# Attention: stacked queries and keys turned by transposing DMAs within SBUF, and a third PSUM bank for scores

## The chip, the cores and the metric

The kernel runs on one core of a Trainium2 chip. Its time is the device time of one execution in microseconds (us); the median of several runs is given. The engines are PE (TensorE, matrix products), DVE (VectorE), ACT (ScalarE), POOL (GpSimd) and SP (SyncE), which here only issues DMAs. SBUF and PSUM are the on-chip memories; PE writes its results to PSUM, which has banks of 2 KB for each of 128 partitions.

## What is computed

A model of four layers on x of shape (16, 256, 256): batch, position, channel. Each layer adds an attention and a feed-forward part. Three of the four attentions, and the self-attention inside the third feed-forward part, are computed by the same function of the kernel. Cut to what matters, each of them is

```
q = split_heads(query)                 # (16, heads, 256, D / heads)
k, v = split_heads(split(memory))
scores = einsum('bhqd,bhkd->bhqk', q, k) + mask or bias of the keys
weights = softmax(scores, axis=-1)
out = einsum('bhqk,bhkd->bhqd', weights, v)
```

with 16 heads of 16 channels or 8 heads of 32; the self-attention is causal.

## The kernel before

The program is a row of stages; each stage has its own buffers and a block in which every engine runs a program of its own, and engines wait for each other by counting semaphores. The change touches `attention_stage` alone, which runs four times: as stage l0a (16 heads, from ctx_2048; it also zeroes two arrays in memory, `clears`), l2a (8 heads), l2s (16 heads, causal) and l3a (8 heads). The calls are in `build`, `self_layer` and `projected_layer`.

The unit of work is a half batch h: 32 of them in each stage, with HALF = heads / 2 heads each (8 or 4). `slots()` is the clock by which all engines' programs are written: j counts half batches, i the head in it, and n = j * HALF + i the head overall. The order of work on an engine is fixed by it; the time at which something runs is set by the waits alone.

- **Stacking (POOL, `stack`).** Scores are to be exact to more than fp16, so each head's query is stacked as high part, high part again and low part, its key as high, low, high; after these 3 * dh rows stand two rows for the bias and one for the row's maximum. Together a head has 64 rows (16 heads) or 128 (8 heads). They lie in `qs` and `ks` (two buffers each), positions on the partitions.
- **Turning (PE, `turn`, L659 to 683).** The product needs these rows on the partitions. PE turns 128x128 blocks against an identity matrix into two PSUM banks, `MH_ps` (in the profile l0a_M and so on): 8 for the queries and 8 for the keys of each half batch, h = j + 2 (TURN_Q_AT and TURN_K_AT). DVE copies the queries (`copy_queries`, L768) into `qT`, ACT the keys (`copy_keys`, L723) into `kT`, at h = j + 1; both are rings of 6 buffers.
- **Scores (PE, `score`, L622)** go to one of two banks `S_ps`, 512 columns a head, and PE waits until the maxima of head n - 2 are done. DVE takes the maxima of the rows (`maxima`, L788; L784 where causal) into `mx`.
- **Maxima back.** Once h = j - 1 is complete, PE turns `mx` (L689), into the first of the two `MH_ps` banks, which it shares with the queries. DVE copies the result to `nmT` (L796), and SP moves it by one DMA (8 heads) or two (16 heads) into a row of `qT` (L513).
- **Scores again, transposed and less the maximum (PE, `scoreT`, L636)**, LAG = heads + 1 heads behind the first ones; ACT takes the exponential (L737), in the causal stage POOL cuts what lies above the diagonal (L581), PE weighs the values (L652) into `O_ps`, ACT copies the sums (L731), PE turns them back (L696), DVE divides (L805, L816).
- **SP's queue** is in the order of the program: the load of keys and values (`kv`, L499) of every second half batch, in l0a the two zeroing DMAs (L506), and the maxima's rows (L513), for which SP waits at each half batch.

## Time and profile before

| | us |
|---|---|
| median of 3 runs | 3162.87 |
| lowest and highest | 3162.02, 3163.29 |
| the profiled execution | 3166.49 |
| its span, first to last instruction | 3164.8 |

The profile is one execution. Its views: the page gives busy time of each engine over the whole span; the busy time by stretch gives the same for chosen intervals, with the clock granted to PE (1.00 is full speed) and the share of the 16 DMA engines' time; the groups of instructions give count, busy us in all and mean ns of one; the waits say which group stood idle until which other one was done. The stages lie at about 65 to 301 us (l0a), 1631 to 1812 (l2a), 1935 to 2156 (l2s) and 2836 to 3019 (l3a), first scores to last products. PEld is PE's weight load, SPq the issue of a DMA on SP. Matmuls overlap, so that the busy time of a group is less than its count times the mean.

### The profile page before, as it was taken

The numbers are of one execution on the slowest core, as the hardware profiler recorded it, in microseconds if no ns is written. First come the engines' busy times: TensorE is split into PE (matmuls) and PEld (weight loads), VectorE is DVE, ScalarE is ACT, GpSimd is POOL, SyncE is SP. The second block draws the span as 40 slices with busy tenths as digits, with TensorE's granted clock in tenths as the row PEclk, the third lists the DMA queues.
The fourth block names the chain that finished last, engine by engine and source line by source line (L and its number), as shares of the span: only waits on it lengthen the run. The fifth ranks groups of instructions, "written<-read, shape, count | busy, mean of one in ns | idle before, by whom it ended". The sixth has DMA issues, their size and how long they took to land. (4 is left out here: it accounts for less than half of the span.)

```text
span 3164.8 us, 57450 instructions
## 1 busy us (share of the span) xinstructions
PE 2533.4 (80%) x21340; PEld 1655.2 (52%) x21340; DVE 2163.2 (68%) x5536; ACT 1307.5 (41%) x2296; POOL 1030.3 (33%) x1446
## 2 busy tenths in 40 slices
PE   1998377999615358997989986897799999969982
PEld 1444264766514136996446553445466555656662
DVE  5997755666477435665578778997766545877767
ACT  1887343343112212332346664773222222356622
POOL 2452371100163520112656467872300000034330
PEclk9999698999857679999999987998799999989996
DMA  3331363233330324775631022100100000011001
GB/s 100 127 128 51 131 235 130 74 104 101 99 92 1 108 96 177 261 250 202 210 120 49 15 84 81 43 23 6 64 9 13 1 1 1 1 39 49 29 9 58
DMA packets 158280, 266.65 MB, mean 84 GB/s; under 512 B 23003, under 2 KB 106249, under 8 KB 151988
## 3 DMA queue, kind: packets, MB, share of 16 engines
q1 hardware_dynamic: 131316, 186.70, 17.8%
q0 software_dynamic: 17904, 76.23, 7.0%
q8 instruction: 172, 2.82, 0.4%
q10 hardware_dynamic: 8784, 0.04, 0.2%
q14 instruction: 104, 0.85, 0.1%
HBM read 174.99 MB, written 88.34 MB: 83 GB/s over the span
## 5 line engine op out<-in xcount | busy, mean ns | idle before, releaser
L1595 ACT ACTIVATE l2e_hf<-l2e_H 128x512 f32<-128x512 f32 x208 | 124.2, 597 | 381.9 <-PE l2e_H L1538 381.9
L1727 POOL TENSOR_TENSOR all_m_rstd<-all_m_sq,all_mhalf 128x8 f32<-128x8 f32 x24 | 39.6, 1650 | 558.7 <-DVE all_m_sq L1712 524.3
L1634 DVE CAST l2e_hh<-l2e_hf 128x512 f16<-128x512 f32 x208 | 92.7, 446 | 122.9 <-ACT l2e_hf L1595 108.7
L788 DVE TENSOR_REDUCE l0a_mx<-l0a_S 128x2 f16<-128x512 f32 x256 | 166.7, 684 | 12.3 <-PE l0a_S L622 10.0
L1538 PE MATMUL l0e_H<-l0e_xT,l0e_w 128*128 128x512 f16 x768 | 168.7, 382 | 0.0
L1538 PE MATMUL l2e_H<-l2o_hi,l2e_w 128*128 128x512 f16 x576 | 151.8, 382 | 15.8 <-DVE l2e_w L1610 15.8
L784 DVE CUSTOM_DVE_ANT_0 l2s_masked<-l2s_S,l2s_mq 128x128 f32<-128x128 f32 (+1 forms) x512 | 153.0, 349 | 16.3 <-PE l2s_S L622 12.1
L737 ACT ACTIVATE l0a_pf<-l0a_ST 128x512 f32<-128x512 f32 x256 | 146.2, 600 | 38.5 <-PE l0a_ST L636 37.4
L1538 PE MATMUL l1e_H<-l1e_xT,l1e_w 128*128 128x256 f16 (+1 forms) x1404 | 158.3, 274 | 3.0 <-DMA l1e_w<-packed,all_second_weight_row 3.0
L1538 PE MATMUL l2e_H<-l2e_hh,l2e_w 128*128 128x512 f16 x640 | 155.1, 379 | 0.0
L1636 DVE TENSOR_TENSOR l2e_hl<-l2e_hf,l2e_hh 128x512 f16<-128x512 f32 x208 | 147.3, 708 | 7.2
L1538 PEld LDWEIGHTS l1e_H<-l1e_xT,l1e_w 128*128 128x128 f16 (+1 forms) x1404 | 143.7, 107 | 15.1 <-DMA l1e_w<-packed,all_second_weight_row 3.3
L737 ACT ACTIVATE l2s_pf<-l2s_ST 128x384 f32<-128x384 f32 x256 | 118.6, 493 | 47.4 <-PE l2s_ST L636 42.9
L1595 ACT ACTIVATE l0e_hf<-l0e_H 128x512 f32<-128x512 f32 x128 | 76.4, 597 | 141.7 <-PE l0e_H L1538 141.7
L2698 POOL DMA_INDIRECT l1n_yb<-results,all_first_read x64 | 63.0, 985 | 203.9 <-POOLq L57 176.8
L1553 PE MATMUL l0e_Y<-l0e_w,l0e_hh 128*128 128x256 f16 x1024 | 124.7, 273 | 0.0
L1538 PEld LDWEIGHTS l0e_H<-l0e_xT,l0e_w 128*128 128x128 f16 x768 | 75.6, 98 | 90.1 <-issue 2.1
L788 DVE TENSOR_REDUCE l3a_mx<-l3a_S 128x2 f16<-128x512 f32 x128 | 88.1, 693 | 40.9 <-PE l3a_S L622 39.8
L581 POOL TENSOR_SCALAR_AFFINE_SELECT l2s_pf<-l2s_pf 128x256 f32<-128x256 f32 x256 | 101.1, 407 | 42.2 <-ACT l2s_pf L737 42.0
L1553 PE MATMUL l2e_Y<-l2e_w,l2e_hh 128*128 128x192 f16 x1024 | 109.4, 248 | 3.5 <-DVE all_x L1650 3.5
L622 PE MATMUL l0a_S<-l0a_kT,l0a_qT 64*128 64x256 f16 x512 | 97.6, 285 | 15.8 <-DVE l0a_mx L788 15.8
L788 DVE TENSOR_REDUCE l2a_mx<-l2a_S 128x2 f16<-128x512 f32 x128 | 87.4, 690 | 29.9 <-PE l2a_S L622 29.1
(706 smaller groups left out, 7262.0 us busy)
## 6 DMA issues: line engine op xcount, KB each, us to landing
l0e_wf<-in_L_ffn_w SPq DMA_DIRECT2D x16, 1024.0 KB, 8.7
rows<-l0a_zeros SPq DMA_DIRECT2D x16, 640.0 KB
l1e_rb<-rows SPq DMA_DIRECT2D x39, 256.0 KB, 8.8
results<-l1e_y SPq DMA_DIRECT2D x39, 256.0 KB, 2.2
l0a_kv<-in_ctx SPq DMA_DIRECT2D x16, 512.0 KB, 4.1
rows<-l0a_zeros SPq DMA_DIRECT2D x16, 512.0 KB
l0d_p_cx<-in_ctx SPq DMA_DIRECT2D x16, 512.0 KB, 7.5
l0e_rb<-rows SPq DMA_DIRECT2D x16, 512.0 KB, 9.7
```

The lines of the kernel that those rows point to most:

```text
L581: nc.gpsimd.affine_select(out=t, in_=t, compare_op=ALU.is_ge, fill=0.0, base=0, pattern=[[0, TB], [1, P]], channel_multiplier=-1).then_inc ...
L622: m = pe.matmul(S_ps[n % 2][:, s_at[u]:s_at[u] + key_to[u]], qT[h % RING][r0:r0 + rows, j, u * P:u * P + P], kT[h % RING][r0:r0 + rows, j, ...
L737: nc.scalar.activation(pf[n % NPF][:, 0:used], ST_ps[n % 2][:, 0:used], ACT.Exp).then_inc(probs, 1)
L784: m = nc.vector.tensor_tensor_reduce(masked[n % 2][u][:, 0:key_to[u]], ps[:, s_at[u]:s_at[u] + key_to[u]], mq[:, S - key_to[u]:S], 1.0, -3 ...
L788: m = nc.vector.tensor_reduce(mx[h % 2][:, :, i], ps[:, :].rearrange("p (u k) -> p u k", u=TB), AX.X, ALU.max)
L1538: mm = pe.matmul(bank[0:fn, :], W[par][0:kn, at + k * wd + f0:at + k * wd + f0 + fn], X, start=(done == 0), stop=(done == k_all - 1))
L1553: mm = pe.matmul(Y[u][:, 0:wd], X[0:kn, k, u * P:u * P + P], W[par][0:kn, at + k * wd:at + (k + 1) * wd], start=(done == 0), stop=(done == ...
L1595: nc.scalar.activation(hf[q % 4][0:fn, :], pair_of(q, lay)[0][0:fn, :], lay.func, scale=1.0 / WS).then_inc(acted, 1)
L1634: nc.vector.tensor_copy(high, v).then_inc(hi_done, 1)
L1636: nc.vector.tensor_tensor(low, v, high, ALU.subtract).then_inc(split, 1)
L1727: self.nc.gpsimd.tensor_tensor(out=(self.rstd, self.rstd2)[which][:, g], in0=(self.sq, self.sq2)[which][:, g], in1=self.g.mhalf[:, 0:self. ...
L2698: nc.gpsimd.indirect_dma_start(yb[n % NB][:, :], None, rows[:, :], bass.IndirectOffsetOnAxis(ap=to.read_row[n % 2][:, n // 2:n // 2 + 1], ...
```

## The change

PE's 16 turns for each half batch go, and so do the copies by DVE and ACT. In their place SP issues four transposing DMAs for h = j + 2, of 128x512 fp16 each, two from `ks` to `kT` and two from `qs` to `qT`. Before them it waits for POOL's stacking, for the landing of the transposes of h - 2, and for the last use of the ring's buffer. POOL waits for the landing of both half batches of batch b - 2 before it stacks into their buffers. The two banks that PE's turns used are split: one becomes a third bank for scores, so that PE waits for the maxima of head n - 3, the other (`N`) holds the turned maxima alone.

```diff
     RING, VR, NPF = 6, 5, 3 * G
-    BACK_AT, MAX_AT, TURN_Q_AT, TURN_K_AT = (1, 2, 5, 7) if heads == 16 else (1, 1, 3, 3)
-    COPY_AT, DIV_AT, KEYS_AT, SUM_AT = (3, 2, 1, 5) if heads == 16 else (2, 3, 1, 3)
+    BACK_AT, MAX_AT, TURN_AT = (1, 2, 5) if heads == 16 else (1, 1, 3)
+    COPY_AT, DIV_AT, SUM_AT = (3, 2, 5) if heads == 16 else (2, 3, 3)
     APART = G // 2 if heads == 16 else 0
...
         ident_h = st.sb("ident_h", [P, P], F16)
-        S_ps = [st.ps(f"S{i}") for i in range(2)]
+        S_ps = [st.ps(f"S{i}") for i in range(3)]
         ST_ps = [st.ps(f"ST{i}") for i in range(2)]
...
         B_ps = [o[:, :, :].rearrange("p s (u q) -> p (s u) q", u=TB) for o in O_ps]
-        MH_ps = [st.ps(f"M{i}", [P, 8, P], F16) for i in range(2)]
-        N_ps = MH_ps[0]
+        N_ps = st.ps("N", [HALF, TB, P], F16)
         if causal:
...
         k_hi, v_set, stacked = st.sem("k_hi"), st.sem("v_set"), st.sem("stacked")
-        chunks, q_turned, k_turned = st.sem("chunks"), st.sem("q_turned"), st.sem("k_turned")
+        k_in = [st.sem(f"k_in{i}") for i in range(2)]
+        q_in = [st.sem(f"q_in{i}") for i in range(2)]
         scored, maxed = st.sem("scored"), st.sem("maxed")
...
             def _(sp):
+                def turn_both(h):
+                    b = h // 2
+                    if h % 2 == 0:
+                        sp.wait_ge(stacked, b + 1)
+                    if h == 0:
+                        sp.wait_ge(q_first, 2)
+                        sp.wait_ge(consts, n_consts)
+                    elif h == 2:
+                        sp.wait_ge(consts, all_consts)
+                    if h >= 2:
+                        sp.wait_ge(q_in[h % 2], h // 2 * 16 * TB)
+                        sp.wait_ge(k_in[h % 2], h // 2 * 16 * TB)
+                    if h >= RING:
+                        sp.wait_ge(scoredT, (h - RING + 1) * HALF)
+                    v = ks[b % 2][:, :, :, :].rearrange("p t h r -> p t (h r)")
+                    for u in range(TB):
+                        sp.dma_start_transpose(kT[h % RING][:, :, u * P:u * P + P],
+                                               v[:, u, h % 2 * 4 * P:(h % 2 + 1) * 4 * P]).then_inc(k_in[h % 2], 16)
+                    v = qs[b % 2][:, :, :, :].rearrange("p t h r -> p t (h r)")
+                    for u in range(TB):
+                        sp.dma_start_transpose(qT[h % RING][:, :, u * P:u * P + P],
+                                               v[:, u, h % 2 * 4 * P:(h % 2 + 1) * 4 * P]).then_inc(q_in[h % 2], 16)
+
                 for j, i, n in slots():
...
                                          ).then_inc(nm_in[h % 2], 16)
+                    if i == TURN_AT and 0 <= j + 2 < NH:
+                        turn_both(j + 2)
                 for i in range(len(clears)):
...
                         else:
-                            pool.wait_ge(chunks, 4 * (b - 1))
+                            for a in range(2):
+                                pool.wait_ge(q_in[a], (b - 1) * 16 * TB)
+                                pool.wait_ge(k_in[a], (b - 1) * 16 * TB)
                         if b:
...
                         if n % HALF == 0:
-                            pe.wait_ge(q_turned, h + 1)
-                            pe.wait_ge(k_turned, h + 1)
-                        if n >= 2:
-                            pe.wait_ge(maxed, n - 1)
-                    m = pe.matmul(S_ps[n % 2][:, s_at[u]:s_at[u] + key_to[u]],
+                            pe.wait_ge(q_in[h % 2], (h // 2 + 1) * 16 * TB)
+                            pe.wait_ge(k_in[h % 2], (h // 2 + 1) * 16 * TB)
+                        if n >= 3:
+                            pe.wait_ge(maxed, n - 2)
+                    m = pe.matmul(S_ps[n % 3][:, s_at[u]:s_at[u] + key_to[u]],
                                   qT[h % RING][r0:r0 + rows, j, u * P:u * P + P],
...
-                def turn(h, i):
-                    v = (qs, ks)[i][h // 2 % 2][:, :, :, :].rearrange("p t h r -> p t (h r)")
-                    for c in range(4):
-                        for u in range(TB):
-                            j = h % 2 * 4 + c
-                            m = pe.transpose(MH_ps[i][:, c * TB + u, :], v[:, u, j * P:j * P + P], ident_h[:, :])
-                    m.then_inc(chunks, 1)
-
-                def turn_queries(h):
-                    b = h // 2
-                    pe.wait_ge(stacked, b + 1)
-                    if b == 0:
-                        pe.wait_ge(q_first, 2)
-                    elif b == 1:
-                        pe.wait_ge(consts, all_consts)
-                    if h >= 3:
-                        pe.wait_ge(nm_rows, h - 2)
-                    if h:
-                        pe.wait_ge(q_turned, h)
-                    turn(h, 0)
-
-                def turn_keys(h):
-                    if h:
-                        pe.wait_ge(k_turned, h)
-                    turn(h, 1)
-
                 def turn_max(h):
                     pe.wait_ge(maxed, (h + 1) * HALF)
-                    pe.wait_ge(q_turned, min(h + 3, NH))
+                    if h:
+                        pe.wait_ge(nm_rows, h)
                     for u in range(TB):
-                        m = pe.transpose(N_ps[0:HALF, u, :], mx[h % 2][:, u, :], ident_h[:, :])
+                        m = pe.transpose(N_ps[:, u, :], mx[h % 2][:, u, :], ident_h[:, :])
                     m.then_inc(nm_turned, 1)
...
                         turn_max(j - 1)
-                    if i == TURN_Q_AT and 0 <= j + 2 < NH:
-                        turn_queries(j + 2)
-                    if i == TURN_K_AT and 0 <= j + 2 < NH:
-                        turn_keys(j + 2)
...
             def _(act):
-                def copy_keys(h):
-                    act.wait_ge(chunks, 2 * h + 2)
-                    nc.scalar.activation(kT[h % RING][:, :, :],
-                                         MH_ps[1][:, :, :].rearrange("p (c u) q -> p c (u q)", c=4), ACT.Copy
-                                         ).then_inc(k_turned, 1)
-
                 def copy_sums(h):
...
                 for j, i, n in slots():
-                    if i == KEYS_AT and 0 <= j + 1 < NH:
-                        copy_keys(j + 1)
                     if i == SUM_AT and 0 <= j - 3 < NH:
...
-                def copy_queries(h):
-                    dve.wait_ge(chunks, 2 * h + 1)
-                    if h >= RING:
-                        dve.wait_ge(scoredT, (h - RING + 1) * HALF)
-                    nc.vector.tensor_copy(qT[h % RING][:, :, :],
-                                          MH_ps[0][:, :, :].rearrange("p (c u) q -> p c (u q)", c=4)
-                                          ).then_inc(q_turned, 1)
-
                 def maxima(n):
...
                         dve.wait_ge(nm_turned, h - 1)
-                    ps = S_ps[n % 2]
+                    ps = S_ps[n % 3]
                     if causal:
...
                         dve.wait_ge(nm_in[h % 2], h // 2 * 16 * per)
-                    nc.vector.tensor_copy(nmT[h % 2][:, :], N_ps[0:HALF, 0:TB, :].rearrange("p u q -> p (u q)")
+                    nc.vector.tensor_copy(nmT[h % 2][:, :], N_ps[:, :, :].rearrange("p u q -> p (u q)")
                                           ).then_inc(nm_rows, 1)
...
                 for j, i, n in slots():
-                    if i == 0 and 0 <= j + 1 < NH:
-                        copy_queries(j + 1)
                     if i == COPY_AT and 0 <= j - 1 < NH:
```

Line numbers of the changed kernel differ: L510 and L514 are its transposing DMAs, L522 the kv load, L536 the maxima's rows, L649 the scores, L663 the transposed scores, L691 the turn of the maxima, L770 and L778 DVE's maxima and their copy.

SP's queue in the middle of l2a, before; L499 is the load of keys and values, L513 the maxima's row:

```order
L513 DMA l2a_qT3<-l2a_nmT1 1x4x256
L513 DMA l2a_qT4<-l2a_nmT0 1x4x256
L499 DMA l2a_kv<-in_ctx_2048 128x2x512
L513 DMA l2a_qT5<-l2a_nmT1 1x4x256
L513 DMA l2a_qT0<-l2a_nmT0 1x4x256
```

and after:

```order
L536 DMA l2a_qT3<-l2a_nmT1 1x4x256
L510 DMA_TRANSPOSE l2a_kT0<-l2a_ks1 128x4x128 x2
L514 DMA_TRANSPOSE l2a_qT0<-l2a_qs1 128x4x128 x2
L536 DMA l2a_qT4<-l2a_nmT0 1x4x256
L510 DMA_TRANSPOSE l2a_kT1<-l2a_ks1 128x4x128 x2
L514 DMA_TRANSPOSE l2a_qT1<-l2a_qs1 128x4x128 x2
L522 DMA l2a_kv<-in_ctx_2048 128x2x512
L536 DMA l2a_qT5<-l2a_nmT1 1x4x256
```

Four transposing DMAs now stand between two rows of maxima. PE in the middle of l2a, before; S are the scores, ST the transposed ones, O the weighed values, M the banks of the turns:

```order
L652 MATMUL l2a_O<-l2a_pf,l2a_va 64x256 x4
L622 MATMUL l2a_S<-l2a_kT,l2a_qT 128x256
L636 MATMUL l2a_ST<-l2a_qT,l2a_kT 128x256
L622 MATMUL l2a_S<-l2a_kT,l2a_qT 128x256
L636 MATMUL l2a_ST<-l2a_qT,l2a_kT 128x256
L664 MATMUL l2a_M<-l2a_ident_h,l2a_qs 128x128 x8
L664 MATMUL l2a_M<-l2a_ident_h,l2a_ks 128x128 x8
L622 MATMUL l2a_S<-l2a_kT,l2a_qT 128x256
L636 MATMUL l2a_ST<-l2a_qT,l2a_kT 128x256
```

and after:

```order
L679 MATMUL l2a_O<-l2a_pf,l2a_va 64x256 x4
L649 MATMUL l2a_S<-l2a_kT,l2a_qT 128x256
L663 MATMUL l2a_ST<-l2a_qT,l2a_kT 128x256
L649 MATMUL l2a_S<-l2a_kT,l2a_qT 128x256
L663 MATMUL l2a_ST<-l2a_qT,l2a_kT 128x256
L649 MATMUL l2a_S<-l2a_kT,l2a_qT 128x256
L663 MATMUL l2a_ST<-l2a_qT,l2a_kT 128x256
```

The 16 turns between two heads' scores are gone; nothing else moved on PE.

## Rows read from the trace of the kernel before

**Rows 1.** Of the page: busy us, share of the span, instructions

```profile
PE 2533.4 (80%) x21340; PEld 1655.2 (52%) x21340; DVE 2163.2 (68%) x5536; ACT 1307.5 (41%) x2296; POOL 1030.3 (33%) x1446
```

**Rows 2.** The busy time by stretch, in l0a, l2a, l2s, l3a

```profile
core 0: us, PE busy (x) PEld busy (x) DVE busy (x) ACT busy (x) POOL busy (x), PEclk, DMA share, GB/s
100.00:280.00 180.00, 169.44 (x2205) 78.03 (x2202) 172.56 (x358) 149.93 (x257) 80.48 (x127) 1.00 0.34 117
1650.00:1790.00 140.00, 138.75 (x1334) 91.97 (x1334) 115.09 (x253) 94.18 (x148) 85.39 (x131) 1.00 0.14 40
1960.00:2130.00 170.00, 153.22 (x2257) 81.23 (x2256) 158.10 (x943) 130.94 (x262) 141.77 (x297) 1.00 0.13 37
2850.00:2990.00 140.00, 140.00 (x1348) 93.03 (x1346) 103.58 (x198) 95.38 (x150) 64.25 (x108) 1.00 0.13 43
```

**Rows 3.** Groups of instructions, l0a; count, busy us, mean ns, idle before

```profile
L788 DVE TENSOR_REDUCE l0a_mx<-l0a_S 128x2 f16<-128x512 f32 x205 | 133.4, 682 | 6.7 <-PE l0a_S L622 5.1
...
L723 ACT ACTIVATE l0a_kT<-l0a_M 128x1024 f16<-128x1024 f16 x26 | 26.4, 1017 | 0.0
...
L768 DVE COPY l0a_qT<-l0a_M 128x1024 f16<-128x1024 f16 x26 | 17.7, 680 | 0.0
```

**Rows 4.** The waits, l0a: who waited for whom, us, times, longest

```profile
PEld l0a_S L622 <- DVE l0a_mx L788: 23.7, 29, 0.9
...
DVE l0a_mx L788 <- PE l0a_S L622: 5.1, 27, 0.2
```

**Rows 5.** Groups of instructions, l2a

```profile
L788 DVE TENSOR_REDUCE l2a_mx<-l2a_S 128x2 f16<-128x512 f32 x99 | 68.0, 691 | 23.0 <-PE l2a_S L622 22.5
...
L664 PE MATMUL l2a_M<-l2a_ident_h,l2a_ks 128*128 128x128 f16 x200 | 15.2, 219 | 0.0
```

**Rows 6.** The waits, l2a

```profile
DVE l2a_mx L788 <- PE l2a_S L622: 22.5, 54, 0.9
PEld l2a_S L622 <- DVE l2a_mx L788: 16.5, 43, 0.4
```

**Rows 7.** Groups of instructions, l2s

```profile
L784 DVE CUSTOM_DVE_ANT_0 l2s_masked<-l2s_S,l2s_mq 128x256 f32<-128x256 f32 x210 | 87.1, 415 | 0.0
L581 POOL TENSOR_SCALAR_AFFINE_SELECT l2s_pf<-l2s_pf 128x256 f32<-128x256 f32 x212 | 83.6, 407 | 28.1 <-ACT l2s_pf L737 28.1
```

**Rows 8.** Groups of instructions, l3a

```profile
L788 DVE TENSOR_REDUCE l3a_mx<-l3a_S 128x2 f16<-128x512 f32 x100 | 69.5, 695 | 34.3 <-PE l3a_S L622 33.3
...
L664 PE MATMUL l3a_M<-l3a_ident_h,l3a_ks 128*128 128x128 f16 x200 | 15.2, 219 | 0.0
```

**Rows 9.** The DMA view, 1700.3 to 1704.3 us; GB/s in 40 slices of 0.1 us

```profile
GB/s 0 0 0 0 0 0 0 0 0 0 0 0 10 10 0 0 0 41 143 266 225 164 82 0 0 20 164 369 389 410 389 410 430 410 389 348 266 184 123 21
DMA packets 279, 0.53 MB, mean 132 GB/s; under 512 B 19, under 2 KB 23, under 8 KB 279
...
q1 hardware_dynamic: 279, 0.53, 45.0%
...
l2a_kv<-in_ctx SPq DMA_DIRECT2D x1, 512.0 KB, 3.7
```

**Rows 10.** The DMA view, 0 to 50 us: packets, MB, share of 16 engines

```profile
q10 hardware_dynamic: 8784, 0.04, 11.9%
```

**Rows 11.** The timeline in l2a: start us, us, engine, line

```profile
1700.35 0.57 SPq L513 DMA_DIRECT2D l2a_qT<-l2a_nmT  x1
...
1700.97 0.44 SPq L499 DMA_DIRECT2D l2a_kv<-in_ctx  x1
...
1704.39 0.10 PEld L636 LDWEIGHTS l2a_ST<-l2a_qT,l2a_kT 128*128 128x128 f16 x1
```

**Rows 12.** The waits of SP's queue

```profile
SPq L513 <- DVE l0a_nmT L796: 163.0, 32, 9.8
...
SPq L513 <- DVE l2a_nmT L796: 149.5, 32, 6.7
```

## The prediction

> **What bounds the kernel now.** I first read the page's busy shares [rows 1]: over the whole span PE is at 80% and DVE at 68%, which says little, because the change touches only the four attention stages. So I read the busy time by stretch, one steady stretch inside each stage [rows 2]. The number of row maxima in a stretch (L788, one for each head; L784 twice) says how many half batches it holds, and that gives the time of one half batch, the "period" below:
> - l0a (16 heads): 205 maxima / 8 = 25.6 half batches in 180 us, 7.03 us each. DVE is busy 172.56 us, 6.74 us each. DVE is the bound; PE has 169.44 us, ACT 149.93.
> - l2s (16 heads, causal): 210 / 8 = 26.25 in 170 us, 6.48 us each. DVE 158.10 us (6.02 each), POOL 141.77 (5.40 each).
> - l2a and l3a (8 heads): 99 / 4 = 24.75 in 140 us, 5.66 us each, and 100 / 4 = 25, 5.60 us. PE is busy 138.75 and 140.00 us, DVE only 4.65 and 4.14 us a half batch. PE is the bound.
> The counts are in [rows 3, 5, 7, 8]. The waits confirm it: in l0a DVE waited for scores only 5.1 us in all, while PE's weight loads waited 23.7 us for maxima [rows 4]; in l2a both wait for each other (DVE 22.5 us for scores, weight loads 16.5 us for maxima [rows 6]), which is what two score banks look like when one engine turns to a long job. Each stage has 32 half batches, so the four together take about 32 × (7.03 + 6.48 + 5.66 + 5.60) = 793 us of the span.
>
> **What is removed.** For each half batch: 16 PE transposes of 128x128 (L664: 15.2 us for the keys in l2a's stretch, and a second row of 15.2 us for the queries, so 30.4 us for 24.75 half batches, 1.23 us each; l3a has the same two rows) [rows 5, 8], one DVE copy of 0.68 us (L768) and one ACT copy of 1.02 us (L723) [rows 3]. Where ACT isn't the bound its copy gives nothing directly. Busy time left to one half batch:
> - l0a: DVE 6.74 − 0.68 = 6.06. Its idle time now is 7.03 − 6.74 = 0.29; I keep it. New period 6.35, gain 0.68.
> - l2s: DVE 6.02 − 0.68 = 5.34, plus idle 0.46 as now, 5.80; POOL's 5.40 lies just under it (L581's cut of each head and the stacking don't change) [rows 7]. Gain 0.68.
> - l2a: PE (138.75 − 30.4) / 24.75 = 4.38; DVE 3.97. PE's busy time hides waits for maxima, 16.5 / 24.75 = 0.67 us of weight loads [rows 6]; the third bank should remove most of them, but the maxima (0.69 us each against some 1.1 us a head) still have to keep pace. I take 4.38 + 0.27 = 4.65, gain 1.01.
> - l3a: PE (140.00 − 30.4) / 25 = 4.38; the same 4.65, gain 0.95.
> Sum: 32 × (0.68 + 0.68 + 1.01 + 0.95) = 32 × 3.32 = 106 us. The third bank has no row of its own. If it gave nothing more than I counted, the two 8-head stages stay about 0.3 us higher (20 us in all); if it removed all idle time, periods would be 6.06, 5.40, 4.20 and 4.20 and the gain 32 × 4.91 = 157 us.
>
> **What is added: four transposing DMAs for each half batch**, 128 x 512 fp16 each, 512 KB together, all on SP's queue. No transposing DMA is in the trace, so its price is a bound from both sides. One 512 KB load took 45.0% of 16 engines in a 4.00 us stretch, so 1.8 us of all engines, with 279 packets: 28.8 us / 279 = 103 ns for a packet of some 1.9 KB [rows 9]. The smallest packets in the trace (queue q10, 8784 packets with 0.04 MB in 50 us at 11.9%) took 95.2 us / 8784 = 10.8 ns each [rows 10]. The transpose reads 512 rows of 256 bytes for each DMA, 2048 for a half batch, 128 for each engine.
> - Low end: only bytes count, 1.8 us a half batch.
> - By the line between the two packet prices: 10.8 + 92 × 256/1900 = 23 ns, 128 × 23 = 3.0 us.
> - High end: each 256-byte row pays a whole large packet's price, 128 × 103 ns = 13.2 us.
> I take 3.0, as an estimate, because a 256-byte row is nearer to the small packets. At 3.0 us it hides in each of the new periods: the queue is otherwise used 0.13 to 0.14 of the time in the 8-head and causal stages and 0.34 in l0a [rows 2], which also zeroes memory. There it comes to 0.34 × 7.03/6.35 + 3.0/6.35 = 0.85 of the engines' time.
>
> The skill bears on this. The trace has no transpose rate; the Trainium skill (DMA: Bandwidth & Descriptors, "Latency and other measured facts") gives 261 GB/s for a transposing DMA, by which 512 KB would take 2.0 us and the sum would stand. No run before shows it.
>
> **SP's side.** SP now issues one DMA of 0.57 us for each half batch in l2a and one of 0.44 us for every second [rows 11]. Four more at 0.44 to 0.57 us add 1.8 to 2.3 us, so SP is at some 3.1 us of 4.65, in the 16-head stages, with two mask-row DMAs (l0a_qT<-l0a_nmT), 3.7 of 5.8. SP spent 149.5 us of l2a and 163.0 of l0a waiting for nmT at L513 [rows 12], so it has the room. Its order matters: the row DMA (nmT into qT) is issued first, the transposes behind it, and the next row DMA stands behind them and behind the kv load. That row DMA gates PE's transposed scores (L636). In l2a it is issued at 1700.35 and its score starts after 1704.4, some 4.0 us later; this shrinks to 3.3 us. Bytes of it move in the slices at 1.2 and 1.3 us of the stretch [rows 9], some 1.2 us behind issue, so about 2 us are needed. The transposes have until the scores two half batches later, over 1.2 periods, at least 5.6 us. Both are covered, with 1 us of slack for the row DMA; if the queue ahead ate that slack in each l0a half batch and 1 us more, it would cost 32 us. New waits on POOL (stacking waits for the landing of the transposes before last, instead of PE's) lie on an engine with slack in l2a and l3a; in l2s POOL has only 0.4 us.
>
> Start and end of a stage: the first half batch now waits some 2 to 4 us for DMAs, as a kv load takes 3.7 us to land [rows 9], instead of PE transposes and copies that take about 2 us, at most 2 us more in each of four stages; in l0a DVE's first copy stood behind memsets, which goes. I count nothing for it, −8 to +8 for the range.
>
> The profiled run took 3166.5 us (span 3164.8, 1.7 around it), 3.6 above the median. 3166.5 − 106 = 3060 beside it, and from the median 3162.9 − 106 = 3057. **Forecast 3057**, own range 3010 to 3100.
>
> **Rivals.**
> 1. *The transposes are slower than the period* (slower than before). Place: the SP queue, the four transposing DMAs, either the issue, which holds SP in proportion to the pieces, or the packets. If they need T us for a half batch, all four stages run at T where it is above their new periods. It turns against the change where 128 × T exceeds 793, at T = 6.2 us, 1.55 us for each DMA. At T = 9.2, between that point and the 13.2 us bound, 3163 + 128 × 9.2 − 793 = 3548; at 13.2, 4060. For it: nothing in the trace shows that a transposed write is as cheap as a read of the same bytes. Against: one packet price holds only for packets seven times larger.
> 2. *Each 128x128 block is a transfer of its own*, one behind another, with the 1.2 us between issue and first byte [rows 9]: 16 × 1.2 = 19 us a half batch, 3163 + 128 × 19 − 793 = 4802. The Trainium skill (VectorE: DVE Perf Modes, "The three transpose paths") has such a price, 1309 ns for a 128x128 block by DMA against 390 by TensorE; 16 of those in a row would give 20.9 us. The trace before doesn't bear it out, since 512 KB loads overlap their fixed part.
> 3. *Queue just in the way*: T between 4.65 and 6.2, or the row DMA is late by a microsecond or two. The 8-head stages keep their old period and the 16-head ones gain in part: 0.68 × 32 × 2 = 44 us, 3120.
> 4. *The change doesn't do what it says*: PE's transposes leave, but DVE and PE stay in step as now, and only the DVE copies' time comes out: 0.68 × 128 = 87 us, 3076; this lies inside the forecast's range and needs no chance of its own.
>
> **How the numbers follow.** Forecast 0.49, rival 3 0.12 (of it 0.02 within 0.2%, about what a measurement of this kernel can tell from no change), rival 1 0.35 (0.21 of it up to T = 9.8), rival 2 0.04. Faster 0.59, same 0.02, slower 0.39. Range: 3010, the gain without idle time, to 3620, T = 9.8 us: it leaves out 0.02 below, and above it 0.14 of rival 1 and rival 2's 0.04.
>
> **What would show it.** Right: in the stretches period 6.35, 5.80, 4.65, 4.65 us by the count of maxima; SP's transposes take under 0.6 us each to issue and land within 5 us; hardly any wait of PE for kT or qT. Rival 1: PE's first score (L622 in before) of each half batch waits for the transposing DMAs, the period is equal in all four stages, and PE, DVE and ACT all fall below 60%. Rival 3: PE's L636 waits for the nmT row. Wrong sizes: a third bank that removes DVE's idle time in l0a (then under 6.2 us), or POOL as the bound in l2s.

## The result and the profile after

The changed kernel took 3350.64 us (median of 4 runs, 3347.96 to 3353.39), the kernel before beside it 3162.44 us: a ratio of 1.059, 95% interval 1.0578 to 1.0603. It is slower by 188 us, where the forecast was faster by 106. The time lies inside the range, on the side of rival 1.

The page, busy us, share and instructions of each engine (as [rows 1]), and the two lines on the queue and the packets:

```profile
PE 2492.3 (74%) x19292; PEld 1564.4 (47%) x19292; DVE 2082.3 (62%) x5408; ACT 1183.0 (35%) x2168; POOL 1025.7 (31%) x1446
...
q1 hardware_dynamic: 409844, 253.88, 28.6%
...
DMA packets 436794, 333.58 MB, mean 100 GB/s; under 512 B 301531, under 2 KB 384777, under 8 KB 430516
```

PE, DVE and ACT all have less work than before [rows 1], as they should. The busy time by stretch in l0a, l2a, l2s and l3a, as [rows 2]:

```profile
100.00:340.00 240.00, 178.50 (x1817) 71.92 (x1819) 159.94 (x333) 126.37 (x234) 85.79 (x136) 0.82 0.61 146
1720.00:1890.00 170.00, 133.24 (x1009) 73.73 (x1007) 103.97 (x240) 77.37 (x133) 90.00 (x141) 0.99 0.58 116
2060.00:2270.00 210.00, 149.37 (x1774) 69.60 (x1774) 138.13 (x886) 100.62 (x229) 137.39 (x289) 0.81 0.46 92
3010.00:3170.00 160.00, 126.08 (x942) 70.07 (x944) 88.53 (x173) 71.97 (x125) 64.12 (x108) 0.98 0.59 119
```

Groups of instructions in l0a and in l2a, as [rows 3, 5]:

```profile
L770 DVE TENSOR_REDUCE l0a_mx<-l0a_S 128x2 f16<-128x512 f32 x208 | 133.0, 684 | 79.1 <-PE l0a_S L649 78.3
...
L770 DVE TENSOR_REDUCE l2a_mx<-l2a_S 128x2 f16<-128x512 f32 x106 | 73.2, 692 | 64.6 <-PE l2a_S L649 64.4
```

208 / 8 = 26 half batches in 240 us are 9.23 us each, 106 / 4 = 26.5 in 170 us are 6.42. No engine of those that compute fills its period now: in l0a PE is busy 74% and DVE 67%, and DVE waits 78.3 us for scores where it waited 5.1 [rows 4]. The periods, and beside them the time from each stage's first maximum to its last, by which all kernels below are compared:

| stage | period before | forecast | after | first to last maximum, before | after |
|---|---|---|---|---|---|
| l0a | 7.03 | 6.35 | 9.23 | 223.5 | 290.5 |
| l2a | 5.66 | 4.65 | 6.42 | 172.9 | 202.4 |
| l2s | 6.48 | 5.80 | 8.27 | 206.5 | 256.1 |
| l3a | 5.60 | 4.65 | 6.40 | 171.1 | 201.7 |

The four grow by 176.7 us together, of the 181.4 by which the span grows (3164.8 to 3346.2). So the loss is in the stages that were changed. **The two 8-head stages** have one period, 6.4 us. What sets it shows in SP's timeline in the middle of l2a (start, duration, line; as [rows 11]):

```profile
1800.31 0.60 SPq L536 DMA_DIRECT2D l2a_qT<-l2a_nmT  x1
1801.03 2.52 SPq L510 DMA_TRANSPOSE l2a_kT<-l2a_ks  x2
1803.59 3.31 SPq L514 DMA_TRANSPOSE l2a_qT<-l2a_qs  x2
1806.95 0.59 SPq L522 DMA_DIRECT2D l2a_kv<-in_ctx  x1
1807.59 0.60 SPq L536 DMA_DIRECT2D l2a_qT<-l2a_nmT  x1
1808.36 2.53 SPq L510 DMA_TRANSPOSE l2a_kT<-l2a_ks  x2
1810.93 2.58 SPq L514 DMA_TRANSPOSE l2a_qT<-l2a_qs  x2
1813.55 0.61 SPq L536 DMA_DIRECT2D l2a_qT<-l2a_nmT  x1
```

From 1800.3 to 1813.6 SP hardly pauses: two half batches in 13.24 us, of which 10.94 us are the eight transposing DMAs; the pauses come to 0.5 us. All 64 of L510 in l2a, duration in ns (smallest, median, largest), and the time from issue to landing:

```profile
L510 SPq DMA_TRANSPOSE l2a_kT<-l2a_ks x64: 1194/1258/2439, 1693.1 to 1892.6; - x64
...
DMA to landing us min/median/max: 2.4/2.5/4.3
```

One holds SP for 1.26 us in the median, and a few for up to 2.4. Over the stretch of 1720 to 1890 us, 26.5 half batches, the transposing DMAs take 142.5 us of SP, 5.4 in each; with the row DMA 0.6, half a kv load 0.25 and pauses of 0.25, that is the period of 6.4 (four at the median would be 5.0). SP's wait for the maxima, 149.5 us in [rows 12], is nearly gone in l2a:

```profile
SPq L536 <- DVE l0a_nmT L778: 43.2, 14, 5.3
...
SPq L536 <- DVE l2a_nmT L778: 7.5, 2, 3.8
```

What PE waits for in l2a, 1720 to 1890 us, is what SP issues late: the transposed queries in front of a half batch's first score, in 23 of 26.5 half batches, and the maxima's rows:

```profile
PE l2a_S L649 <- DMA l2a_qT<-l2a_qs: 24.0, 23, 2.2
...
PE l2a_ST L663 <- DMA l2a_qT<-l2a_nmT: 12.7, 11, 1.6
```

**The 16-head stages** run above what SP needs, and there SP still waits (43.2 us in l0a). The waits in l0a, 100 to 340 us, as [rows 4] (who waited for whom: us, times, longest):

```profile
DVE l0a_mx L770 <- PE l0a_S L649: 78.3, 49, 5.2
...
PE l0a_ST L663 <- DMA l0a_qT<-l0a_nmT: 58.9, 13, 5.3
```

PE stands in front of the transposed scores until the maxima's rows have landed, 13 times in 26 half batches, so in every second one, by 58.9 / 13 = 4.5 us. Spread over all 26 that is 2.3 us each, as much as the period has grown (2.2). In every second half batch SP's queue also holds a kv load and, in l0a only, the DMAs that zero memory, between the transposes and the next row. In l2s, 2060 to 2270 us:

```profile
PE l2s_O L679 <- POOL l2s_pf L608: 55.5, 19, 6.2
POOL l2s_qs L571 <- DMA l2s_qT<-l2s_qs: 55.4, 12, 6.5
```

POOL waits at L571, before it stacks the next batch, for the landing of the transposes that read the same stacks, 12 times, 4.6 us each. Behind that on POOL are the causal cuts (L608), and PE waits for these just as long.

### The profile page after: what moved, and what is told of

Read it like the earlier page. It is cut to its first block and busy times, and to the rows that moved or that the text cites. A ratio compares the mean times of both kernels' runs of the same rounds, so it can differ in the third digit from the quotient of the medians.

```text
span 3346.2 us, 53606 instructions
## 1 busy us (share of the span) xinstructions
PE 2492.3 (74%) x19292; PEld 1564.4 (47%) x19292; DVE 2082.3 (62%) x5408; ACT 1183.0 (35%) x2168; POOL 1025.7 (31%) x1446
## 3 DMA queue, kind: packets, MB, share of 16 engines
q1 hardware_dynamic: 409844, 253.88, 28.6%
## 5 line engine op out<-in xcount | busy, mean ns | idle before, releaser
L770 DVE TENSOR_REDUCE l0a_mx<-l0a_S 128x2 f16<-128x512 f32 x256 | 163.5, 685 | 99.0 <-PE l0a_S L649 98.1
L729 ACT ACTIVATE l0a_pf<-l0a_ST 128x512 f32<-128x512 f32 x256 | 142.9, 601 | 159.2 <-PE l0a_ST L663 158.9
L649 PE MATMUL l0a_S<-l0a_kT,l0a_qT 64*128 64x256 f16 x512 | 111.5, 313 | 74.6 <-DMA l0a_qT<-l0a_qs 72.0
L663 PE MATMUL l0a_ST<-l0a_qT,l0a_kT 64*128 64x256 f16 x512 | 104.8, 307 | 68.7 <-DMA l0a_qT<-l0a_nmT 68.1
L770 DVE TENSOR_REDUCE l3a_mx<-l3a_S 128x2 f16<-128x512 f32 x128 | 88.0, 693 | 92.5 <-PE l3a_S L649 92.5
L770 DVE TENSOR_REDUCE l2a_mx<-l2a_S 128x2 f16<-128x512 f32 x128 | 87.8, 691 | 83.0 <-PE l2a_S L649 82.8
L679 PE MATMUL l2s_O<-l2s_pf,l2s_va 128*32 128x256 f32 (+1 forms) x1024 | 80.7, 394 | 62.2 <-POOL l2s_pf L608 60.9
L649 PE MATMUL l2s_S<-l2s_kT,l2s_qT 64*128 64x256 f16 (+1 forms) x512 | 93.8, 283 | 37.4 <-DMA l2s_qT<-l2s_qs 32.0
```

The lines of the kernel that those rows point to most:

```text
L649: m = pe.matmul(S_ps[n % 3][:, s_at[u]:s_at[u] + key_to[u]], qT[h % RING][r0:r0 + rows, j, u * P:u * P + P], kT[h % RING][r0:r0 + rows, j, ...
L663: m = pe.matmul(ST_ps[n % 2][:, t_at[u]:t_at[u] + S - query_from[u]], kT[h % RING][r0:r0 + rows, j, u * P:u * P + P], qT[h % RING][r0:r0 + ...
L679: m = pe.matmul(O_ps[h % 2][lane * vw:(lane + 1) * vw, w % 2, query_from[c]:S], va[b % VR][:, c, n % heads, :], pf[n % NPF][:, t_at[c]:t_a ...
L729: nc.scalar.activation(pf[n % NPF][:, 0:used], ST_ps[n % 2][:, 0:used], ACT.Exp).then_inc(probs, 1)
L770: m = nc.vector.tensor_reduce(mx[h % 2][:, :, i], ps[:, :].rearrange("p (u k) -> p u k", u=TB), AX.X, ALU.max)
```

## The experiments

The kernel before took about 3161 us beside some of these runs and 3080 beside the others, so each is compared by its ratio to the kernel before that ran beside it. The 80 us lie between l0a and l2a, in stages that the change doesn't touch: from l0a's last maximum to l2a's first it is 1341.8 us in the profile of before, 1332 to 1343 in all runs of the first kind and 1250 to 1265 in those of the second (zero_last apart). The times of the four stages can therefore be set side by side, one profile each. The runs of the second kind are rows_act, wide, wide_rows, late_stack, zero_last, split and he_two_banks. Where no interval is given (sizes, late_stack, zero_last), the kernel ran once.

**Half of the change each.** Only the queries, or only the keys, are turned by DMA; the others go through PE, a PSUM bank and a copy as before.

```
# q_dma, cut to what matters (k_dma the other way round: qs through PE and DVE's copy)
-                    for u in range(TB):
-                        sp.dma_start_transpose(kT[h % RING][:, :, u * P:u * P + P], ...)
+                            m = pe.transpose(M_ps[:, c * TB + u, :], v[:, u, j * P:j * P + P], ident_h[:, :])
+                    nc.scalar.activation(kT[h % RING][:, :, :], M_ps..., ACT.Copy).then_inc(k_turned, 1)
```

> Only the queries are turned by transposing DMAs (two for each half batch); the keys go through PE and ACT's copy as before, the third score bank stays. Theory A (SP's sequencer is held 1.27 us by each transposing DMA and is the bound): SP needs 2 x 1.27 + 0.6 + 0.3 = 3.4 us of a half batch with 8 heads and about 4.4 with 16, below the other engines, so the periods are about 6.4 (l0a), 5.9 (l2s), 5.1 and 5.1 us (l2a, l3a) and the time about 3085 us, faster than before. Theory B (each transposing DMA costs a share of its own through the shared queue, so half of them cost half): about 3163 + 188/2 = 3257 us.

> Only the keys are turned by transposing DMAs; the queries go through PE and DVE's copy as before, third score bank kept. Theory A: SP is no bound here either; DVE keeps its 0.68 us copy, so the 16-head stages stay near 7.0 and 6.4 us, the 8-head stages fall to about 5.1; about 3163 - 32 x (0.55 + 0.5) = 3130 us. Theory B: 3257 us as with the queries.

Measured: q_dma 3149.8 us, 0.9968 (0.9956 to 0.998); k_dma 3150.5 us, 0.9964 (0.9949 to 0.9978). With half of the transposes the loss of 5.9% is a gain of 0.3%, so it is not in proportion, as it would be if every transposing DMA cost the same. In l2a the stage takes 162.6 and 160.0 us, against 172.9 before; by the count of maxima, 100 and 101 from 1650 to 1780 us, that is 5.2 us a half batch, where 5.1 had been expected. But l0a takes 236.1 and 239.9 us, over the 223.5 of before, and l2s 205.2 and 207.1, as before; the expected 3085 and 3130 were missed there. In q_dma, l0a, 100 to 280 us:

```profile
PE l0a_ST L660 <- DMA l0a_qT<-l0a_nmT: 23.3, 11, 4.7
```

Even two transposes make the rows late by 2.1 us in 11 half batches.

**Two score banks instead of three.** With the bank go its place in the ring of scores and PE's wait, which is for the maxima of head n - 2 again.

```
-        S_ps = [st.ps(f"S{i}") for i in range(3)]
+        S_ps = [st.ps(f"S{i}") for i in range(2)]
```

> The changed kernel with two banks for scores in place of three, nothing else. Theory A: SP bounds the 8-head stages and late DMAs the 16-head ones, so the bank matters little: 3350 to 3370 us. Rival C (the third bank lets PE run ahead and is itself part of the loss): clearly below 3350 us.

Measured: 3342.1 us, 1.0564 (1.0545 to 1.0584), against the change's 1.059 (1.0578 to 1.0603). The intervals overlap: the third bank is neither the cause nor a help that can be measured while SP sets the period.

**What one transposing DMA costs.** A stage ahead of the kernel issues them alone, each after the one before has landed, on blocks of 128x128; then eight of 4 blocks in a row. This adds work and nothing is left out.

```
+                for n in (1, 2, 4, 8, 16, 32, 1, 2, 4, 8, 16, 32):
+                    sp.dma_start_transpose(dst[:, 0:n, :], src[:, 0:n * P]).then_inc(landed, 16)
+                    k += 1
+                    sp.wait_ge(landed, 16 * k)
```

> The changed kernel with a stage in front of the load that issues transposing DMAs of 1, 2, 4, 8, 16, 32 blocks of 128x128 fp16 one by one (twice), then plain copies of 128x512, 128x2048, 128x4096 within SBUF, then eight of 4 blocks in a row. If the hold on SP is a fixed price, each takes about 1.27 us on SP whatever its size; if it goes by the block, it is about 0.3 us a block, 10 us for 32 blocks. Landing: by packets, 3.0 us of all engines for 16 blocks, so about 2 us fixed and 0.19 us a block.

Measured (SP's timeline; 1, 4, 8, 16 and 32 blocks, and the eight in a row):

```profile
3.08 1.22 SPq L3005 DMA_TRANSPOSE probe_dst<-probe_src  x1
...
7.75 1.20 SPq L3005 DMA_TRANSPOSE probe_dst<-probe_src  x1
...
10.17 1.23 SPq L3005 DMA_TRANSPOSE probe_dst<-probe_src  x1
...
13.25 1.32 SPq L3005 DMA_TRANSPOSE probe_dst<-probe_src  x1
...
17.54 4.84 SPq L3005 DMA_TRANSPOSE probe_dst<-probe_src  x1
...
54.59 10.37 SPq L3014 DMA_TRANSPOSE probe_dst<-probe_src  x8
```

The hold on SP is 1.2 us for 1 block and for 8, so it is paid for the instruction, not for the data. From one issue to the next (landing between them) it was 2.3 us for 1 block, 2.4 for 4, 3.1 for 8, 4.3 for 16 and 6.7 for 32. From 16 to 32 blocks 2.4 us buy 16 blocks of 32 KB: 0.150 us a block, 218 GB/s. The eight in a row took 10.37 us, 1.30 each, for 128 KB each: 101 GB/s, half of what the queue can move. **So with 4 blocks to a DMA the issue limits, not the packets**, and a DMA of 8 blocks costs SP what one of 4 does. At 32 blocks the hold is 4.8 us, so beyond 8 it grows.

**Eight blocks to a DMA, in two ways.** wide turns both half batches of a batch with four DMAs, issued once a batch. halves keeps the moment, two DMAs each half batch, and lays the stacks out so that the blocks of a half batch lie side by side.

```
# wide, its place in SP's queue
-                    if i == TURN_AT and 0 <= j + 2 < NH:
-                        turn_both(j + 2)
+                    if i == TURN_AT and j % 2 == 0 and 0 <= j + 2 < NH:
+                        turn_batch((j + 2) // 2)
# halves, the layout (qs the same way)
-        ks = [st.sb(f"ks{i}", [P, TB, heads, rows], F16) for i in range(2)]
+        ks = [st.sb(f"ks{i}", [P, 8, TB, per, rows], F16) for i in range(2)]
```

> Both tensors turned by DMA as in the changed kernel, same bytes and blocks, but four DMAs of 8 blocks (128x1024) for each batch of two half batches instead of eight of 4 blocks. Theory A (a hold on SP of about 1.25 us for each DMA, whatever its size up to 8 blocks): SP's share halves to 2.5 us a half batch, the 8-head stages fall from 6.4 to about 4.7 us; l0a, whose rows of maxima still stand behind the kv load and the zeroing in one queue, to about 7.4, l2s to about 6.0 since POOL waits for an older batch; about 3350 - 240 = 3110 us. Theory B (the engines' time for the packets or the bytes counts): same bytes, no change, 3350.

> The changed kernel with qs and ks laid out so that a half batch's 8 blocks lie in a row: two transposing DMAs of 8 blocks for each half batch in place of four of 4, at the same place in SP's queue, same bytes. Theory A (each holds SP about 1.3 us whatever it carries, up to 8 blocks): SP's work falls from 6.0 to about 3.5 us in the 8-head stages, whose 202 us from the first to the last maxima fall to 31 x 4.8 = 150; l0a from 290 to about 235 and l2s from 256 to about 210, as with two DMAs of 4 blocks. In all 0.98 of before. Theory B (bytes or packets bound): 1.059 as the changed kernel.

Measured: wide 3096.8 us, 1.0045 (1.0033 to 1.0058); halves 3153.9 us, 0.9975 (0.9962 to 0.9987). The same bytes as in the change and 98% of the queue's packets (401652 in both for 409844), half of the instructions, and the 5.9% are nearly or wholly gone either way. The queue's share is not smaller (31.1% of 3156.0 us in halves, 28.6% of 3346.2 in the change), so it is the number of instructions that counts. Both stay above what had been expected, 0.983 (3110 us) and 0.98. In halves, DMAs and SP's wait for the maxima:

```profile
L509 SPq DMA_TRANSPOSE l2a_kT<-l2a_ks x32: 1237/1260/2235, 1644.2 to 1793.7; - x32
...
L509 SPq DMA_TRANSPOSE l2a_qT<-l2a_qs x32: 1253/1335/1993, 1645.5 to 1795.0; - x32
```

```profile
SPq L532 <- DVE l2a_nmT L774: 42.8, 29, 4.2
```

SP has room again (29 waits instead of 2) and l2a takes 154.2 us, l3a 152.9. In wide l2a takes 181.6: all four DMAs of a batch stand ahead of its first half batch, the queries' last, and there PE's scores waited for qT in every batch (19.4 us, 11 times, 1570 to 1700 us). But halves has l0a at 248.1 and l2s at 216.2, both over before, so SP's load is not all that holds up the 16-head stages: rows and stacks are late there too. wide has l0a at 209.1, below before; why it does so much better there than halves was not tested.

**Rows through another queue.** The maxima's rows are issued by ACT, one head later, in the change (rows_act) and in wide (wide_rows). ACT waits for the maxima and for the landing of the half batch's queries before it issues them.

```
-                            sp.dma_start(qT[h % RING][row:row + 1, 0:HALF // per, :], nmT[h % 2][a:HALF:per, :]
+                        act.dma_start(qT[h % RING][row:row + 1, 0:HALF // per, :], nmT[h % 2][a:HALF:per, :]
```

> The changed kernel, but the small DMAs that move the maxima's rows (nmT into qT) are issued by ACT on its own queue instead of SP. If late rows make l0a's period 9.2 us and SP's hold the 8-head ones 6.4, l0a falls to about 6.6, l2a and l3a to about 5.5 (5.1 + 0.3 us of SP), l2s stays near 8 because POOL's wait for landings is untouched: about 3350 - 157 = 3193 us. If the rows aren't late by the queue, nothing changes.

> Both of these edits: 8-block DMAs and the rows on ACT's queue. Neither SP's hold nor the queue order is left, so the periods should be those of the prediction's sum, 6.4, 5.9, 4.7, 4.7 us: about 3070 us. If something else about transposing DMAs costs time, it shows here as a rest above 3100.

Measured: rows_act 3164.7 us, 1.0276 (1.0259 to 1.0293), l0a 248.9 us and l2a 186.8; wide_rows 3109.3 us, 1.0088 (1.0071 to 1.0105). The first halves the loss, since SP is rid of 0.6 to 1.2 us a half batch and the rows stand behind none of SP's DMAs. Both miss what had been expected, about 1.01 (3193 us) and 0.97 (3070). With the rows gone SP still has hardly a pause in l2a: from 1600 to 1740 us its transposes hold it for 129 us and the loads for 6, 5.7 us a half batch, where 5.4 had been expected. wide_rows is over wide as a whole, but not everywhere: the 8-head stages are faster by it (164.4 and 160.6 us for 181.6 and 179.3), the 16-head stages slower (234.7 and 224.3 for 209.1 and 210.8). There ACT now waits for the maxima, and the exponentials behind the issue are late. In rows_act, l0a, 100 to 300 us:

```profile
PE l0a_ST L656 <- ACT l0a_pf L722: 28.2, 25, 1.5
```

**The stacks in l2s.** late_stack stacks two heads later on POOL, so that the landing has time; early issues the transposes at the first head of a half batch (TURN_AT 0 for 5 and 3).

```
# late_stack
-                    part = (j % 2 * HALF + i) // 2
+                    part = (j % 2 * HALF + i) // 2 - 1
...
# early
-    BACK_AT, MAX_AT, TURN_AT = (1, 2, 5) if heads == 16 else (1, 1, 3)
+    BACK_AT, MAX_AT, TURN_AT = (1, 2, 0) if heads == 16 else (1, 1, 0)
```

> The changed kernel with POOL's stacking in the causal stage moved two heads later, nothing else. If POOL's wait for the transposes' landing holds up the cuts queued behind it (62 us of PE waiting for L608 in 25 half batches of l2s), l2s falls from 8.3 to about 7.5 us a half batch, 3350 - 26 = 3324 us; the other stages don't change. If l2s is slow for another reason (rows, clock), nothing changes.

> The changed kernel with the transposes issued at the start of the half batch and nothing else. SP's hold is unchanged, so the 8-head stages stay SP-bound at about 6.3 us a half batch (200 us each); the 16-head stages gain where rows and POOL were late: l0a from 290 to about 250, l2s from 256 to about 225 us; 1.035 of before. If the order is of no matter, 1.059.

Measured: late_stack 3248.0 us, 1.054, l2s 238.2 us; early 3296.8 us, 1.0429 (1.0409 to 1.0449), l2s 228.4 and l0a 273.0 us. POOL's wait was real: of the 49.6 us that l2s lost, 18 come back by the one and 28 by the other. In late_stack POOL's waits for the landing are shorter but not gone (37.6 us, 12 times, 3.1 each, 1980 to 2160 us), and 26 us had been expected. In early l2s comes near the expected 225 us; l0a misses its 250, and PE still waits there for the rows (44.1 us, 14 times, 100 to 330 us). The 8-head stages stay at 203 to 206 us in both, as they must if SP's four issues set them.

**Both, on the kernel with few instructions.** halves_early is halves with the early issue; halves_late has late_stack's line too; he_two_banks is halves_early with two score banks.

> As halves, and the transposes for two half batches ahead are issued at the start of a half batch, ahead of SP's wait for the maxima's rows, so that the rows find an empty queue and the landing is earlier for POOL. If late rows and POOL's wait are what is left in the 16-head stages, l0a falls to about 210 us and l2s to about 190, in all 0.965 of before. If the order in the queue doesn't matter, the same as halves.

> As halves_early, and POOL's stacking in the causal stage two heads later. If POOL still waits for landings in l2s, another 5 to 10 us off it; if not, no change within 0.1%.

> halves_early with two score banks instead of three. If the third bank matters once SP isn't the bound, the 8-head stages lose some 0.3 us a half batch, 10 us each, and the whole is 0.992 of before or more; if it doesn't, 0.986.

Measured: halves_early 3114.6 us, 0.9856 (0.9836 to 0.9877), l2s 188.2 us against halves' 216.2, as expected; but l0a 232.5, where 210 had been expected, so the whole misses its 0.965. halves_late 3141.5 us, 0.9938 (0.9921 to 0.9956): a miss, l2s goes back to 214.3, and what was late is now a row (1960 to 2140 us):

```profile
PE l2s_ST L659 <- DMA l2s_qT<-l2s_nmT: 28.0, 10, 4.0
```

What SP waits for ahead of these rows is not the stacks (2.4 us) but POOL's copy of the values, which stands behind the stacking and has to be done before SP issues the next kv load. Over 1925 to 2130 us:

```profile
SPq L518 <- POOL l2s_va L593: 29.0, 11, 2.7
```

In halves_early it was 10.4 us. So a delay on POOL is handed through the load to the rows queued behind it. he_two_banks 3043.7 us, 0.9874 (0.9859 to 0.989): its interval overlaps that of halves_early, and l2a and l3a take 157.5 and 150.2 us for 156.3 and 151.0, so the third bank gives nothing that can be measured even where SP is free.

**What makes the rows late in l0a.** zero_last issues the zeroing DMAs behind everything else of l0a, in the change; split is halves_early with one of the two zeroing DMAs in each half batch instead of both in every second.

```
# split
-                    if clears and i == 0 and j % 2 == 0 and 0 <= b < B:
+                    if clears and i == 0 and 0 <= b < B:
-                        for c, m, done in zip(clears, per_step, cleared):
+                        for c, m, done in [list(zip(clears, per_step, cleared))[1 - j % 2]]:
```

> The changed kernel with all 32 zeroing DMAs of l0a issued at the end of the stage's queue instead of two with every kv load; the maxima's span of l0a is what is to be read, the whole time grows by the 60 to 80 us in which the zeroing runs alone. If the rows of maxima are late because they stand behind the zeroing, l0a's span falls from 290 to about 220 us (SP's 5.1 + 1.2 + 0.3 us a half batch). If l0a is slow because of the transposing DMAs alone, it stays above 270.

> halves_early with the two zeroing DMAs of l0a in alternating half batches instead of both beside the kv load. Same bytes. If the rows are late in every second half batch by what stands ahead of them, l0a's span falls from 232 to about 215 us and the whole to 0.980 of before; if only the sum of bytes counts, 0.986 as halves_early.

Measured: zero_last 3242.7 us, 1.053, l0a 237.2 us against 290.5 (220 had been expected); PE still waits for the rows, 20.9 us in 180. All of it does not reach the total, because the zeroing then runs alone at the end: from l0a's last maximum to l2a's first it is 1289 us, some 30 more than in the other runs of its kind. split 3015.8 us, **0.9799 (0.9785 to 0.9812)**, l0a 213.4 us, and this beats both kernels. PE's waits for the rows, halves_early and then split, both 100 to 280 us:

```profile
PE l0a_ST L659 <- DMA l0a_qT<-l0a_nmT: 23.0, 11, 3.6
```

```profile
PE l0a_ST L659 <- DMA l0a_qT<-l0a_nmT: 16.2, 11, 3.0
```

The kernels side by side, first to last maximum in us:

| kernel | l0a | l2a | l2s | l3a | ratio |
|---|---|---|---|---|---|
| before | 223.5 | 172.9 | 206.5 | 171.1 | 1 |
| the change | 290.5 | 202.4 | 256.1 | 201.7 | 1.059 |
| two_banks | 291.4 | 201.7 | 257.7 | 203.6 | 1.0564 |
| q_dma | 236.1 | 162.6 | 205.2 | 158.9 | 0.9968 |
| k_dma | 239.9 | 160.0 | 207.1 | 160.0 | 0.9964 |
| rows_act | 248.9 | 186.8 | 223.2 | 186.0 | 1.0276 |
| wide | 209.1 | 181.6 | 210.8 | 179.3 | 1.0045 |
| wide_rows | 234.7 | 164.4 | 224.3 | 160.6 | 1.0088 |
| late_stack | 291.1 | 205.6 | 238.2 | 203.2 | 1.054 |
| early | 273.0 | 203.3 | 228.4 | 203.2 | 1.0429 |
| zero_last | 237.2 | 203.5 | 254.3 | 202.0 | 1.053 |
| halves | 248.1 | 154.2 | 216.2 | 152.9 | 0.9975 |
| halves_early | 232.5 | 156.3 | 188.2 | 151.0 | 0.9856 |
| halves_late | 233.8 | 157.6 | 214.3 | 150.5 | 0.9938 |
| he_two_banks | 235.0 | 157.5 | 192.1 | 150.2 | 0.9874 |
| split | 213.4 | 156.5 | 190.8 | 153.3 | 0.9799 |

## Why the prediction was wrong, step by step

- **What bounds the kernel now** held. The maxima's counts gave the periods, and the loss lies in these four stages alone.
- **What is removed** was right in kind: PE's 16 turns and the two copies went. Its worth was too high. With SP, rows and stacks mostly out of the way (split) the four stages take 714.0 us against 774.0, a gain of 60 of the 106 us. In split's l2a, 1540 to 1680 us, PE is the bound again: it is busy 133.9 of 140 us, and 113 maxima make a half batch 4.96 us, of which PE is busy 4.74, where 4.38 had been worked out. 1.23 us had been subtracted for the 16 turns, as the sum of two groups; in the timeline of before they overlap and take 1.06 us together (1701.94 to 1703.00 us). The other 0.2 us stay open. In l0a rows are still late (16.2 us).
- **The packets' price** came out right, and part of that is luck: it was read off a straight line between two packets of other kinds. The one queue was busy 28.6% of 3346.2 us, before 17.8% of 3164.8: 394 us over 128 half batches, 3.08 us each, where 3.0 had been taken between bounds of 1.8 and 13.2. The rate of the Trainium skill that stood beside it (DMA: Bandwidth & Descriptors, "Latency and other measured facts", 261 GB/s, given there for a pattern that is not contiguous) is some 20% above the 218 GB/s of the probe.
- **SP's side is the step that failed.** "Four more at 0.44 to 0.57 us" took the price of plain DMAs, 1.8 to 2.3 us; each transposing DMA held SP 1.27 us in the median, 5.1 a half batch, and 5.4 with the longer ones. SP was to be at 3.1 of 4.65 us and was full at 6.4. That is the loss of the 8-head stages, 60 of the 177 us; the 16-head stages have the other 117, by the next two points, and there too part of it is SP's load, since halves, with half of the instructions, brings back 82 of them. With 5.1, the prediction's own sum gives 5.1 + 0.6 + 0.3 = 6.0 us, above the 4.65 forecast and above the 5.66 of before. By the rivals as written it would still have passed as rival 3, because rival 1's break-even, 6.2 us or 1.55 for each DMA, counts the transposes alone. With the 1.3 us that rows, loads and pauses take of SP's 6.4, the break-even of the 8-head stages lies near (5.6 − 1.3) / 4 = 1.1 us for each DMA, as an estimate. Of the two mechanisms that rival 1 named for its place it was the issue, but by the instruction and not "in proportion to the pieces": 1.20 us for 4 blocks, 1.23 for 8. The nearest row was taken as the price, though it was of another kind of instruction, and was not given a range of its own.
- **"Both are covered, with 1 us of slack for the row DMA"** failed as well. In l2a PE waited for the rows 12.7 us in 26.5 half batches, and for the transposed queries 24.0. In l0a the slack was taken by the transposes and the zeroing in front of the rows, 4.5 us every second half batch; the text had priced one microsecond, 32 us, left it out of the forecast, and l0a lost 67.
- **The new waits on POOL.** They were named, with "POOL has only 0.4 us" in l2s, and not priced; POOL waited 4.6 us 12 times, and l2s lost 50. The cuts queued behind the waiting stack were named nowhere.
- **Start and end of a stage**, counted as nothing, held: the span grew by 4.7 us outside the four stages.
- **The third bank** counted for about 0.3 us in the 8-head stages. Two pairs of runs show no gain from it.
- **Rival 1**'s first sign, PE's first score waiting for the transposing DMAs, showed in the 8-head stages. It gave an equal period in all four stages; it was equal only in these two (6.42 and 6.40). PE did not fall below 60%: it was busy 78% of l2a's stretch and 74% of l0a's. **Rival 2** is out: a DMA of 4 blocks lands in 2.5 us, not in 4 × 1.2. The price beside it, 1309 ns for a block (the Trainium skill, VectorE: DVE Perf Modes, "The three transpose paths"), differs from the probe both ways: 2.3 us for a block alone, from its issue to the next one's behind its landing, and 0.15 us in a long transfer. **Rival 3**'s late rows came true, in l0a at over twice the microsecond or two it allowed; its 3120 us did not.
- **Left open:** PE ran at a granted clock of 0.82 in l0a and 0.81 in l2s, where it had 1.00 [rows 2], a mean between its two levels (1.2 and 2.4 GHz), in stretches in which PE stood 4.5 us (for rows) or 2.9 us (for cuts) at a time. In l0a the products with the values (L679) took 438 ns in the mean for 391 before. The share of that in the 67 and 50 us was not separated from the waits themselves, though the waits alone have the size of the loss. In halves_early l0a had 0.90, in split 0.98.

## What to carry to other kernels

Moving work from an engine to a DMA queue moves its cost to the instruction that issues it: count issues per period and take the hold of that very kind of DMA, or leave its price open up to where it would decide. Make such DMAs few and large (8 blocks cost the issuing engine what 1 does), and look at which small, urgent DMA stands behind them in the same queue. An engine that waits for a landing holds back everything queued behind the wait, so ask for those and not only for the engine's mean load.

## What the runs showed of the hardware

- A transposing DMA within SBUF held SP's queue 1.1 to 1.2 us for 1 to 8 blocks of 128x128 fp16 (sizes), 1.3 to 1.8 for 16 and 4.8 for 32; in the kernel 4 blocks held it 1.26 us in the median and up to 2.6. A plain DMA within SBUF of 128 partitions held it 0.47 to 0.57 (sizes).
- It moved 218 GB/s in long transfers, and 101 GB/s when issued 4 blocks at a time, eight in a row. The plain copies of the same probe took 1.5 us for 512 KB more, 345 GB/s.
- With the small row DMAs issued by ACT instead of SP (rows_act), PE waited 28.2 us in 200 us of l0a for ACT's exponentials.
